# Counting destination digits with comparisons against constants, in groups of twelve ids

## The reference

```python
edge_index = jnp.stack([src, dst])
x = _layernorm(x + gnn0(x, src, dst, ...))         # means over edges, then a GRU cell
x = _layernorm(x + gnn1(x, edge_index, edge_attr)) # messages, summed by src
# in gnn0
a_in  = _seg_mean(feat_in[src], dst, N)
a_out = _seg_mean(feat_out[dst], src, N)
```

## Time and profile before

| | us |
|---|---|
| median of 3 runs | 13825.87 (13824.88 to 13830.94) |
| span of the profiled execution | 13804.0 |
| median less span | 21.9 |
| first stage, up to the first read of the second | 125.06 |
| of it the loop of 30 steps on VectorE | 12.66 to 113.99 |

### The profile page before, as it was taken

The page is one execution under the profiler, slowest core; times in us unless marked ns, Lnnn a source line. Parts: engine busy times, 40 slices in busy tenths (PEclk is TensorE's granted clock), DMA queues, the critical chain, the costliest instruction groups (busy, mean ns, idle before and its releaser), DMA issues. The chain is left out here.

```text
span 13804.0 us, 248896 instructions
## 1 busy us (share of the span) xinstructions
PE 8659.3 (63%) x53687; PEld 7672.6 (56%) x53688; DVE 8365.0 (61%) x29393; ACT 2711.9 (20%) x7251; POOL 9686.8 (70%) x10125
## 2 busy tenths in 40 slices
PE   3777775333333333333577777797878888888886
PEld 2555554333333333333577777556777777777775
DVE  6555555666666666666677777654444455444444
ACT  0000000111111111111000000153444444444443
POOL 3777775777777777777777777306777777777774
PEclk9555555555555565656788888898999999999998
DMA  5822222666666666666677767513333334333336
GB/s 179 307 54 54 54 54 69 199 200 197 200 197 198 198 198 198 198 199 197 175 186 187 187 182 189 101 45 81 79 80 79 80 88 95 80 80 79 80 80 82
DMA packets 2665835, 1886.18 MB, mean 137 GB/s; under 512 B 1375879, under 2 KB 2460455, under 8 KB 2664868
## 3 DMA queue, kind: packets, MB, share of 16 engines
q1 hardware_dynamic: 1505354, 806.75, 22.0%
q0 software_dynamic: 377360, 782.89, 19.5%
q10 hardware_dynamic: 782662, 292.60, 8.7%
HBM read 1509.53 MB, written 483.44 MB: 144 GB/s over the span
## 5 line engine op out<-in xcount | busy, mean ns | idle before, releaser
L1806 POOL DMA_INDIRECT p<-q_rows,small x3432 | 3241.7, 945 | 1645.7 <-issue 1001.8
L1011 PE MATMUL bank<-p,ring 128*128 x6656 | 1551.7, 427 | 2740.1 <-DVE ring L958 2736.8
L1011 PEld LDWEIGHTS bank<-p,ring 128*128 128x128 f32 x6656 | 1439.3, 328 | 2852.5 <-issue 2852.4
L1070 POOL DMA_INDIRECT edges_a<-ring,small x1664 | 1633.9, 982 | 593.1 <-issue 455.7
L1070 POOL DMA_INDIRECT edges_b<-ring,small x1664 | 1631.9, 981 | 507.2 <-issue 450.5
L805 POOL DMA_INDIRECT ring<-in_x,ring x1664 | 1569.9, 943 | 533.4 <-issue 530.1
L1844 PE MATMUL bank<-ring 128*128 128x256 f32 x3432 | 1199.8, 435 | 761.0 <-DVE p L1756 758.9
L836 PE MATMUL bank<-ring 128*128 128x129 f32 x3328 | 1239.5, 491 | 613.9 <-DMA ring<-in_x,ring 542.1
L1212 POOL DMA_INDIRECT ring<-in_x,small x1352 | 1275.8, 944 | 467.6 <-issue 409.1
L1232 PE MATMUL bank<-p,ring 128*128 128x129 f32 x8360 | 1217.2, 316 | 539.0 <-DVE ring L1160 538.9
L1232 PEld LDWEIGHTS bank<-p,ring 128*128 128x128 f32 x8360 | 1179.7, 230 | 577.3 <-issue 577.2
(11 more groups left out here) (285 smaller groups left out, 13425.4 us busy)
## 6 DMA issues: line engine op xcount, KB each, us to landing
p<-rows_by_slot SPq DMA_DIRECT2D x418, 928.0 KB
p<-edges_b SPq DMA_DIRECT2D x530, 262.0 KB
p<-edges_a SPq DMA_DIRECT2D x520, 262.0 KB
bonds_by_dst<-in_bond ACTq DMA_DIRECT2D x5, 20625.0 KB, 159.9
ring<-edges_a ACTq DMA_DIRECT2D x1792, 33.0 KB
p<-q_rows,small POOLq DMA_INDIRECT x3432
ring<-edges_b ACTq DMA_DIRECT2D x1664, 33.0 KB
ring<-bonds_by_dst ACTq DMA_DIRECT2D x1672, 32.0 KB
```

The source lines that it names most:

```text
L1011: last = nc.tensor.matmul(found[q][:, j, :], hot_t[g % GRPS][:, QUAD * h + j, :], x, start=True, stop=True, skip_group_check=True)
L1070: pool.indirect_dma_start(out=c.edges[s], out_offset=bass.IndirectOffsetOnAxis(ap=pos[:, k:k + 1], axis=0), in_=rec[:, k, :], in_offset=No ...
L1806: pool.indirect_dma_start(out=gath[g][:, k, :], out_offset=None, in_=c.q_dram, in_offset=bass.IndirectOffsetOnAxis(ap=gidx[g][:, k:k + 1], ...
```

## The change

The digits are taken once for all 3300 ids, as int32 (`whole`), cast to bf16 by ACT (`digits`), and compared with constants, one comparison for each value of each digit: 13 + 8 = 21 for a step. A step is now 660 ids, in 55 groups of 12, and the tiles hold, for each group, value after value, twelve ids side by side. So there are 5 steps, 105 comparisons and 5 x 55 = 275 products of 96 columns of weights (`vs`) by 156 moving columns (`us`). The loops are written out. VectorE takes the digits before anything else, ACT casts them before it issues its loads, and the comparison of neighbours stands ahead of the count; its sum is made by TensorE as ten products with a column of ones and one short reduction.

```diff
-HC, CG = 110, 5
+HC, CG = 660, 12
-    after = scratch[:, 7000:7000 + TT // 2].bitcast(BF16)
+    after = c.blk_s[0:TP, 0:TT]
+    us = [scratch[...].bitcast(BF16).rearrange("p (g d t) -> p g d t", d=HU, t=CG) for n in range(2)]
+    vs = [at.bitcast(BF16).rearrange("p (g d t) -> p g d t", d=HV, t=CG) ...]
         def _(act):
             act.dma_start(c.consts[:, :], ins["consts"]).then_inc(s_const, 16)
+            for k in range(2):
+                act.wait_ge(s_digit, k + 1)
+                nc.scalar.copy(digits[k], whole[k]).then_inc(s_cast, 1)
...
         def _(dve):
             step = Chain(dve, s_step)
+            dve.wait_ge(s_ids[1], 32)
+            nc.vector.tensor_scalar(whole[0], raw[:, 1, 0:TT], 10, None, ALU.logical_shift_right).then_inc(s_digit, 1)
+            nc.vector.tensor_scalar(whole[1], raw[:, 1, 0:TT], 7, 7, ALU.logical_shift_right,
+                                    ALU.bitwise_and).then_inc(s_digit, 1)
...
-            with dve.Fori(0, HSTEPS // 2) as i:
-                    step.mark(nc.vector.tensor_scalar(digits[0], ids, 10, None, ALU.logical_shift_right))
-                    step.link(nc.vector.tensor_scalar(digits[1], ids, 7, 7, ALU.logical_shift_right, ALU.bitwise_and))
-                        nc.vector.tensor_tensor(
-                            hot, dig.unsqueeze(2).to_broadcast([TP, HC, width]),
-                            c.iota[0:TP, 0:width].unsqueeze(1).to_broadcast([TP, HC, width]),
-                            ALU.is_equal).then_inc(s_dig, 1)
+            dve.wait_ge(s_edge, 16)
+            nc.vector.tensor_tensor(after, raw[:, 1, 0:TT], raw[:, 1, 1:TT + 1], ALU.is_gt).then_inc(s_viol, 1)
+            dve.wait_ge(s_cast, 2)
+            for i in range(HSTEPS):
+                n = i % 2
+                if i >= 2:
+                    dve.wait_ge(s_cnt, i - 1)
+                for dig, hot, width in ((digits[0], us[n], HU), (digits[1], vs[n], HV)):
+                    for d in range(width):
+                        nc.vector.tensor_scalar(hot[:, :, d, :], dig[:, i * HC:(i + 1) * HC].rearrange("p (g t) -> p g t", t=CG),
+                                                float(d), None, ALU.is_equal).then_inc(s_dig, 1)
...
-            step.link(nc.vector.tensor_tensor(after[:, 0:TT], raw[:, 1, 0:TT], raw[:, 1, 1:TT + 1], ALU.is_gt))
-            nc.vector.reduce_sum(viol, after[:, 0:TT], AXX).then_inc(s_viol, 1)
+            step.link(nc.vector.reduce_sum(viol, c.bank[2][0:1, 0:HC // 2], AXX))
...
         def _(pe):
+            for i in range(HSTEPS):
+                n = i % 2
+                pe.wait_ge(s_dig, (HU + HV) * (i + 1))
+                for t in range(APART):
+                    last = nc.tensor.matmul(cross, vs[n][:, t, :, :].rearrange("p d t -> p (d t)"),
+                                            us[n][:, t, :, :].rearrange("p d t -> p (d t)"),
+                                            start=(i == 0 and t == 0), stop=(i == HSTEPS - 1 and t == APART - 1))
+                last.then_inc(s_cnt, 1)
+            pe.wait_ge(s_viol, 1)
+            for t in range(0, TT, HC // 2):
+                last = nc.tensor.matmul(c.bank[2][0:1, 0:HC // 2], c.ones[0:TP, 0:1], after[:, t:t + HC // 2],
+                                        start=(t == 0), stop=(t == TT - HC // 2))
             pe.wait_ge(s_cross, 1)
             for t in range(CG):
+                last = nc.tensor.matmul(counts, cross_s[:, t:CG * HU:CG], c.ident[0:CG * HV, t:CG * HV:CG],
+                                        start=(t == 0), stop=(t == CG - 1))
```

More of the change, by code:

```diff
@@ L51 @@
 assert MIX >= HALF + QPS and (QSTEPS + 1) * MIX <= S_COLS
-HC, CG = 110, 5
+HC, CG = 660, 12
 HSTEPS = TT // HC
-assert HSTEPS * HC == TT and HSTEPS % 2 == 0 and HC % CG == 0 and CG * HU <= P
+assert HSTEPS * HC == TT and HC % CG == 0 and CG * HV <= P and CG * HU <= 512
+APART = HC // CG
 PT = 10
@@ L223, in load_constants_and_count @@
     s_cross = c.sem("cross_copied")
+    s_digit, s_cast = c.sem("digits_taken"), c.sem("digits_cast")
     scratch = c.p3_flat[0:TP, :]
@@ L226, in load_constants_and_count @@
     pairs = c.pairs()
-    after = scratch[:, 7000:7000 + TT // 2].bitcast(BF16)
[L228 to L232, removed]
+    after = c.blk_s[0:TP, 0:TT]
+    digits = [scratch[:, 6610 + k * (TT // 2):6610 + (k + 1) * (TT // 2)].bitcast(BF16) for k in range(2)]
+    top = 6610 + TT
+    whole = [scratch[:, top + k * TT:top + (k + 1) * TT].bitcast(I32) for k in range(2)]
+    us = [scratch[:, top + n * (HC * HU // 2):top + (n + 1) * (HC * HU // 2)].bitcast(BF16)
+          .rearrange("p (g d t) -> p g d t", d=HU, t=CG) for n in range(2)]
+    vs = [at.bitcast(BF16).rearrange("p (g d t) -> p g d t", d=HV, t=CG)
+          for at in (c.part(7200, HC * HV // 2)[0:TP, :], c.tab[0:TP, 0:HC * HV // 2])]
+    assert top + HC * HU <= (NB + 1) * XW and 7200 + HC * HV // 2 <= RINGW and HC * HV // 2 <= S_COLS
     spare = 2 * TT
@@ L236, in load_constants_and_count @@
     nothing = c.part(spare + REC + D + 8, REC)
-    cross, counts = c.bank[0][0:CG * HU, 0:CG * HV], c.bank[1][0:HU, 0:HV]
-    cross_s = c.small[0:CG * HU, 64:64 + CG * HV]
+    cross, counts = c.bank[0][0:CG * HV, 0:CG * HU], c.bank[1][0:HU, 0:HV]
+    cross_s = c.small[0:CG * HV, 64:64 + CG * HU]
     cs = c.small[0:HU, 0:HV]
-    viol = c.small[0:TP, 32:33]
+    viol = c.small[0:1, 32:33]
     pad_ids = c.small[:, 40:42].bitcast(I32)
@@ L286, in _ @@
             act.wait_ge(s_const, 16)
+            act.wait_ge(s_cast, 2)
         @block.gpsimd
@@ L311, in _ @@
             nc.vector.tensor_copy(c.iota_b[:, :], c.iota).then_inc(s_z, 1)
-            dve.wait_ge(s_ids[1], 32)
-            with dve.Fori(0, HSTEPS // 2) as i:
[L314 to L317, removed]
-                    step.mark(nc.vector.tensor_scalar(digits[0], ids, 10, None, ALU.logical_shift_right))
-                    step.link(nc.vector.tensor_scalar(digits[1], ids, 7, 7, ALU.logical_shift_right, ALU.bitwise_and))
-                    for dig, hot, width in ((digits[0], us[n], HU), (digits[1], vs[n], HV)):
-                        nc.vector.tensor_tensor(
-                            hot, dig.unsqueeze(2).to_broadcast([TP, HC, width]),
-                            c.iota[0:TP, 0:width].unsqueeze(1).to_broadcast([TP, HC, width]),
-                            ALU.is_equal).then_inc(s_dig, 1)
-                    dve.wait_ge(s_dig, 4 * i + 2 * n + 2)
@@ L326, in _ @@
-            step.end(HSTEPS // 2)
+            dve.wait_ge(s_edge, 16)
[9 more added lines that the diff above has]
+                                                float(d), None, ALU.is_equal).then_inc(s_dig, 1)
@@ L327, in _ @@
+            dve.wait_ge(s_cnt, HSTEPS)
+            nc.vector.tensor_copy(cross_s, cross).then_inc(s_cross, 1)
             dve.wait_ge(s_cntd, 1)
-            nc.vector.tensor_copy(cross_s, cross).then_inc(s_cross, 1)
-            dve.wait_ge(s_cntd, 2)
             nc.vector.tensor_copy(cs, counts).then_inc(s_cs, 1)
-            dve.wait_ge(s_edge, 16)
-            step.link(nc.vector.tensor_tensor(after[:, 0:TT], raw[:, 1, 0:TT], raw[:, 1, 1:TT + 1], ALU.is_gt))
-            nc.vector.reduce_sum(viol, after[:, 0:TT], AXX).then_inc(s_viol, 1)
@@ L334, in _ @@
             dve.wait_ge(s_flag, 1)
-            nc.vector.tensor_copy(c.flag[:, 0:1], c.bank[2][0:1, 0:1]).then_inc(s_cs, 1)
-            nc.vector.tensor_scalar(c.flag[:, 1:2], c.bank[2][0:1, 0:1], 1.0, float(E + P), ALU.min, ALU.mult).then_inc(s_cs, 1)
+            step.link(nc.vector.reduce_sum(viol, c.bank[2][0:1, 0:HC // 2], AXX))
+            nc.vector.tensor_copy(c.flag[:, 0:1], viol).then_inc(s_cs, 1)
+            nc.vector.tensor_scalar(c.flag[:, 1:2], viol, 1.0, float(E + P), ALU.min, ALU.mult).then_inc(s_cs, 1)
@@ L340, in _ @@
         def _(pe):
-            pe.sem_inc(s_cnt, 1)
             pe.wait_ge(s_z, 8)
[L343 to L352, removed]
@@ L353, in _ @@
-            nc.tensor.matmul(cross, zero16[:, 0:1].to_broadcast([TP, CG * HU]),
-                             zero16[:, 0:1].to_broadcast([TP, CG * HV]), start=False, stop=True).then_inc(s_cntd, 1)
+            for i in range(HSTEPS):
[6 more added lines that the diff above has]
+                last.then_inc(s_cnt, 1)
@@ L355, in _ @@
+            pe.wait_ge(s_viol, 1)
+            for t in range(0, TT, HC // 2):
+                last = nc.tensor.matmul(c.bank[2][0:1, 0:HC // 2], c.ones[0:TP, 0:1], after[:, t:t + HC // 2],
+                                        start=(t == 0), stop=(t == TT - HC // 2))
+            last.then_inc(s_flag, 1)
             pe.wait_ge(s_cross, 1)
             for t in range(CG):
-                last = nc.tensor.matmul(counts, c.ident[0:CG * HU, t * HU:(t + 1) * HU],
-                                        cross_s[:, t * HV:(t + 1) * HV], start=(t == 0), stop=(t == CG - 1))
+                last = nc.tensor.matmul(counts, cross_s[:, t:CG * HU:CG], c.ident[0:CG * HV, t:CG * HV:CG],
```

(3 more changed lines are left out.)

## The result

The changed kernel is slower: 13886.59 us (13877.85 to 13905.74, 5 runs) against 13825.87, a ratio of 1.0046 with an interval of 1.0035 to 1.0057. The forecast was 13777.1 and 0.35% faster; the range ended at 13801.

The account below looks back on a forecast made before the run. VectorE's comparisons were taken to bound the first stage; its end moves from 125.06 to 76.3 us, saving 48.8. Span 13804.0 becomes 13755.2, plus 21.9 around it 13777.1 us; range 13752 to 13801.

Parts of the forecast that it names:

- a shift of the start moves these stages without changing them: Gathering and message stages: GpSimd sets its own pace, 226.6 to 226.9 us of gathers per 300, whatever the clock.
- what the first stage saves should arrive at the end one for one: Whole kernel: barriers separate the stages, so the first stage's 48.8 us should come off the total in full.
- the one rival that lost the gain later: Later stages: some transfer has a later start anyway and absorbs the gain; 13800 to 13826, chance 0.05.
- Start of the count: First stage: the count starts at 21.5 us, after ACT's table load and two copies; VectorE is free at 20.6.
- the three prices: First stage's 105 comparisons: 0.26, 0.52 or 1.04 ns per element; 0.52 taken, 0.413 us each, 43.4 together.
- A price for each short row: First stage's comparisons: 1 ns per row, 0.055 us each, 5.8 us together; left out of the sum.
- Products: First stage, TensorE: 85 ns each from weight loads, 4.7 us per step; only the last step shows, 4.9 us.
- Tail: End of first stage: ten products 1.5 us, small products 0.8, counts' copy 0.25, store 2.9, barrier 1.0.
- The ids' store: First stage: SP issues it at 43 to 49 us; it lands at 53 to 60, hidden under SP's last wait.
- Comparisons at 0.26 ns: First stage rival: 0.242 us per comparison, next stage reads at about 59.5, 65.6 us saved, 13760.3; chance 0.17.
- Those at 1.04 ns: First stage rival: pairing is also refused on short rows, 36 us more, 12.8 saved, 13813.1; chance 0.09.
- the clock in the node update: Node update rival: TensorE left at half clock, stretches take twice as long, 14077 if all 300 us do; chance 0.03.

Follow-up runs that it names:

- The first experiment: Kernel before plus 88 never-executed memsets in VectorE's program, in the sort's branch not taken: 13933.93 us against 13816.34, ratio 1.0085.
- +16: Changed kernel plus 16 never-executed memsets in VectorE's program, in the sort's branch not taken: 13750.42 us, ratio 0.9953 to the kernel before.
- +144: Changed kernel plus 144 never-executed memsets in VectorE's program, in the sort's branch not taken: 13773.36 us, ratio 0.9951 to the kernel before.

## Why the prediction was wrong

**The step that failed** is in the first part: "a shift of the start moves these stages without changing them", and from it that "what the first stage saves should arrive at the end one for one". I had asked whether other work or the clock tied the later stages to the start, and rightly found not. I had not asked whether the edit changed the later stages themselves. It did, by making VectorE's program 88 instructions longer. The sum had no term for it, no rival was built on it, and the one rival that lost the gain later rested on a late transfer. The first experiment measured that loss by itself, 117.6 us. With it put in, the 48.8 saved become a loss of 68.8, and 60.7 was measured.

The signs were in the trace of before, which I had not looked at: the 1.9 and 3.6 us of "issue" once a turn, and 266 packets of instructions from 2400 to 6600 us, where six were enough from 150 to 2200, in and ahead of the first gathering stage, whose loop of 276 stays.

The Trainium skill has the rule (Runtime: NRT & Kernel Launch, Instruction fetch mechanics): an engine's instruction memory is refilled in blocks, prefetch only runs forward, and a taken branch to a block that is no longer held stalls for its fetch. The runs agree with that: the fetches come once a turn, and VectorE goes on 1.9 us behind a packet's start. The Trainium skill gives 32 KiB (512 instructions) in blocks of 16 KiB, 256 instructions. Here the packets are of 8 KB. In the changed kernel the long wait comes some four instructions into the loop, so with +16 the head stands about 12 places behind that border. The loop of 365 listed instructions stayed there and was fetched again with 28. If the border is one of blocks of 256, two of them would have held the loop in both cases; if it is the middle of such a block, they would have held it in the kernels before and after, which fetched it (266 and 262 packets). Three blocks of 128, 384 places, hold it with 12 and not with 28 (377 against 393), and with +144 as with +16, as measured. So the measurement speaks for blocks of 128, of which three serve a loop, with the reserve that the listing may miss an instruction here or there. The loop of 451 was fetched in all runs, the one of 276 in `sum_in_first` in none, as three such blocks would have it.

**The first stage, by the terms.**
- Start of the count: 21.86, forecast 21.5. ACT's casts ended at 19.6, as its table was loaded at 1.31, under the wait. VectorE itself was later, as the comparison of neighbours waited 1.1 us for its transfer. So the forecast of ACT as the last was wrong, and the 21.5 nearly came out by another path.
- The first shift was forecast for the end of GpSimd's fill, 12.0; it starts at 11.91, and the profile names the ids' transfer as the releaser. Which of the two held it was not tried.
- Comparisons: 0.403 us apart, forecast 0.413, 42.4 us together where I had 43.4. The choice between the three prices was right, and the reason is narrower than the one given: not every unlike division costs a doubling, as L619 shows, and with 66 rows in place of 55 it comes back, at 0.241 (forecast for that rival 0.242). A price for each short row, kept for the range, did not show. The row it came from, L1390, has its rows of three where it reads; it writes one run.
- Products: 98 and 69 ns apart in turn, forecast 85. The last step took 5.6, forecast 4.9. The rate behind it, 0.87 ns per column of weights, would give 111 ns for the 128 columns of the earlier trace rows, for which the prediction itself read 57: it was no rate that holds for all widths.
- Tail: ten products 1.57 (1.5), 24 records of small products 0.79 (0.8). The store and the barrier took 2.2 from 72.28 to 74.43 where I had 3.9.
- The ids' store went out at 34.18, forecast 43 to 49. ACT's loads were issued from 15.6 on, beside its casts, and the issue of 6 us took 0.6 this time. Hidden, as said.
- The read of the counts: 74.43, forecast 76.3.

**The rivals.** Comparisons at 0.26 ns did not happen in this kernel, and did with 66 rows. Those at 1.04 ns did not happen. The slower rival, the clock in the node update, is refuted: the stretch from the last gather of `sum_rest` to the first of `messages` is 554.2 against 549.5, and 551.6 in the first run, the slowest of all. Slower had 0.03; the mechanism that brought it was not on the list.

**Also wrong:** 21.9 us around the span. It was the distance of the profiled execution, a short one, from the median. It did not matter for the sign, as the saving was taken as a difference. And the parts named beside the sum don't add up to it: 101.3 - 43.4 + 3.6 - 9.5 is 52.0, not 48.8. The 48.8 is the difference of the two reads of the counts, and that stands.

## What to carry to other kernels

An edit that lengthens an engine's program moves all loops behind it, and can change their time. Before writing out a loop, look in the trace for waits for "issue" that come once a turn and for the packets of the instruction queue by stage; a stage that is fetched each turn is sensitive to where its loop begins, and a few instructions in a branch that is not taken can be worth more than the edit. When a saving of 50 us goes missing, compare the lengths of all stages, not the stage that was edited.

For one-source comparisons in bf16 whose two sides divide differently, try an even number of rows first: 66 rows of 10 cost a third less than 55 of 12.

## What was not expected of the hardware

- Dead code moved a 13.8 ms kernel by +117.6 us (+88 places) and by -16.0 us (+104 places).
- The refetching itself costs little when the block behind the head comes in time: `sort_records` took 4278.8 to 4295.7 us in the four profiles with 261 to 266 packets and no long wait, and 4273.4 to 4284.6 in the four with 8 to 13. The stall at the border costs more, 34 to 40 us there and 88 to 91 in `sum_rest`.
- The 55 products of a step take 5.5 to 5.6 us or 4.0 in turn. In the changed kernel the granted clock is 0.72 from 47 to 53 us and from 64 to 70, each time with TensorE idle for 4.5 us ahead, and 1.00 from 56 to 60, with 2.9 us of idle time ahead; 0.72 is a mean over the two levels. The first step takes 5.5 at a clock of 1.00, and this was not cleared up.
